# VectorE adds the fourth key tile to the sum of probabilities, and the row sums become one group of matmuls

## The chip, the cores and the metric

The kernel runs on one core of one Trainium2 chip. The metric is the device time of one execution in microseconds, as the median of the runs shown. The core has TensorE (matrix products, PE in the profile), VectorE (DVE), ScalarE (ACT), GpSimd (POOL) and the queue engine SyncE (SP), which here only starts transfers. They share the on-chip memory SBUF; matmuls write to eight accumulator banks, the PSUM (tile PS), which GpSimd does not use in this kernel.

## The reference, cut to what matters

The reference is a decoder layer over 4 sequences of 512 rows by 512 columns, in fp32: self attention, cross attention to a context of width 128 with a causal mask, and a feed-forward part with 2048 hidden columns and gelu. Each part starts with a layer norm and adds its result to x. Both attentions have 16 heads of 32 columns.

```python
q = hidden_states @ wq.T + bq          # k and v alike
scores = einsum('bhsd,bhtd->bhst', q, k) * scale
new_max = max(scores); new_exp = exp(scores - new_max)
output = einsum('bhst,bhtd->bhsd', new_exp, v) / sum(new_exp)
x = x + output @ wo.T + bo             # self attention
...
scores = where(causal, qh @ kh.T * inv_sqrt_d, min)   # cross attention
x = x + softmax(scores) @ vh @ Wout.T
x = x + gelu(layernorm(x) @ proj1.T + b1) @ proj2.T + b2
```

In self attention the loop of four ring steps sees the same keys each time, so one step gives the same result. In cross attention the causal mask leaves only the first 512 of the 1601 context rows in use.

## The kernel before

**Units.** Attention is worked in 32 units `u`: one unit is one sequence and one group of four heads (`HPG`). Units 0 to 15 are the self layer, 16 to 31 the cross layer; with four groups per sequence, `b, g = divmod(u, GROUPS)`. Projections are exact products of split operands: each fp32 operand is split into a high and a low part and `product` issues three matmuls (lines 1000 to 1002).

In a unit, TensorE makes the scores twice. `scores_for_max` (L1106) makes them with queries on the partitions, for the unit to come, and VectorE takes each row's maximum (`maximum`, L1350 in the self layer, L1356 with the mask in the cross layer). `transpose_max` (L1134) turns the maxima, `copy_max` (ScalarE, L904) puts them into the stack of queries, and `scores` (L1123, the mask at L1126) makes the scores again with keys on the partitions and the maximum subtracted. ScalarE takes the exponential into `PT` (L919). The key rows are four tiles of 128, `k` = 0 to 3. `PT` has eight slots, and tile `k` of head `h` lies in slot `(4k + h) % 8`, so tiles 2 and 3 overwrite tiles 0 and 1. In the cross layer, tile `k` holds the queries from `128k` on only.

`weigh_values` (L1139) multiplies each key tile by the values, four heads side by side in the array, and counts `p_used`. For the sum of each row of probabilities, GpSimd adds tile 0 and tile 1 of each head into `P_sum` (L783) and then tile 2 (L789). `sum_rows` then issues two groups of four heads at L1139: ones against `P_sum`, and ones against tile 3 in `PT`. VectorE's `divide` takes the reciprocal (L1364) into `oT`, which is the place of the fourth head in `P_sum`, and multiplies the weighted values by it (L1366). ScalarE (`high_output`, L892) and GpSimd (`low_output`, L773) split the result for the output projection, and GpSimd may overwrite `P_sum`'s fourth head after that.

**Order.** Each engine works in order. For TensorE, ScalarE and VectorE the order in a unit is sorted from the table `PLACES`: places in units of about a microsecond for every unit's scores, weighted values, maxima, projections' pieces (`fill`), the turn of the maxima (`body` + 1), the row sums (`body` + 2), the statistics of a coming norm, the division of the unit before, and the split of its output. `act_order`, `dve_order` and `sp_order` derive their places from TensorE's; SP's queue stores Q and K to a scratch tensor in memory and loads them back as stacks at those places. GpSimd's order is written out by hand: raw weights placed before 3.0, adds of tile 1 with `low_output` before the third, raw weights up to 9.0, adds of tile 2, the other raw weights, then the roots of the norm and the bias adds. The eight banks are dealt out in TensorE's order (`bank_fills`), with the estimates `FREED` of how long each kind is held after its place.

**Waits that matter here.** `sum_rows` waits for GpSimd's adds of the unit (`p_added`) and its last matmul counts the unit's fourth `p_used`; the division waits for it. The exponentials of tile 0 wait for the adds of the unit before, those of tile 1 for the unit before's sums (the fourth `p_used`), those of tile 2 for the adds of tile 1. VectorE's feed-forward work includes `split_hidden` (L1437, L1439), GpSimd's `ffn` bias adds at L842.

Of the kernel before, what the change touches and what calls it, by code (L numbers as in the profile page):

```python
# [7 lines left out]
BF16 = mybir.dt.bfloat16  # L8
# [4 lines left out]
P = 128  # L13
# [86 lines left out]
ADD_HEADS = {SELF: 1, CROSS: 2}  # L100


def adds_before(u):

    cross = max(u - FIRST_CROSS, 0)
    return (u - cross) * 2 * HPG + cross * (HPG + HPG // ADD_HEADS[CROSS])


def adds_until(u, k, h):

    return adds_before(u) + (h + 1 if k == 1 else HPG + h // ADD_HEADS[layer_of(u)] + 1)


BANKS = 8
FREED = dict(T=0.11, S=0.83, M=2.33, G=1.3, R=4.16, O=5.65)
# [3 lines left out]
RAW_PLACES = ((0, 0.01, 5.17, 11.56), (14.3, 22.85), (31.55,), (3.64, 24.47, 17.66, 13.33), (13.15,))  # L119
# [3 lines left out]
CHUNK_PLACES = [(25, (2.12, 13.03)), (26, (5.91, 10.57)), (28, (6.61, 7.41)), (28, (13.83, 14.58)), (29, (10.94, 19.45)), (30, (9.47, 16.47))]  # L123
# [7 lines left out]
    SELF: (dict(body=22.32,  # L131
                scores=((0.08, 0.7), (2.33, 0.39), (5.66, 1.1), (9.16, 1.52)),
                values=(4.1, 4.44, 12.02, 17.56),
                maxima=(2.5, 13.9, 18.4),
                fill=(-1.06, 13.51, 23.02),
                stats=17.28,
                divide=-2.47,
                output=3.81),
           dict(body=28.99,
                scores=((0, 0.02), (3.69, 0.66), (5.67, 1.2), (9.93, 0.32)),  # L140
                values=(5.89, 5.92, 12.1, 17.39),
                maxima=(4.36, 9.15, 16.64),
                fill=(-1.0, 11.58, 28.83),
                stats=9.24,
                divide=0.28,
                output=5.61),
           dict(body=18.49,
                scores=((1.41, 0.34), (2.65, 0.14), (7.74, 0.91), (10.49, 1.06)),
                values=(5.54, 5.81, 18.56, 18.74),
                maxima=(4.56, 9.84, 15.63),  # L150
                fill=(1.0, 9.85, 16.32),
                stats=-6.27,
                divide=0.32,
                output=3.16),
           dict(body=33.95,
                scores=((1.31, 0.22), (2.69, 0.64), (4.82, 0.87), (9.84, 1.24)),
                values=(6.17, 9.49, 11.36, 21.68),
                maxima=(3.6, 13.39, 16.85),
                fill=(1.09, 12.94, 22.75),
                stats=5.72,  # L160
                divide=0.32,
                output=4.14)),
    CROSS: (dict(body=22.71,
                 scores=((0.06, 0.51), (2.49, 0.79), (5.12, 1.59), (8.55, 0.02)),
                 values=(5.58, 8.61, 8.84, 11.87),
                 maxima=(5.17, 7.73, 19.33),
                 fill=(1.83, 10.03, 22.33),
                 stats=7.39,
                 divide=2.71,
                 output=4.29),  # L170
            dict(body=27.59,
                 scores=((0.07, 0.37), (2.29, 0.38), (5.5, 1.11), (7.82, 0.7)),
                 values=(3.5, 5.38, 11.23, 11.6),
                 maxima=(2.14, 5.48, 13.28),
                 fill=(-2.83, 7.99, 14.02),
                 stats=-5.83,
                 divide=-3.2,
                 output=3.13),
            dict(body=14.89,
                 scores=((0, 0.25), (1.66, 0.61), (6.12, 0.97), (9.01, 0.57)),  # L180
                 values=(5.23, 5.63, 10.4, 12.22),
                 maxima=(3.42, 6.65, 8.52),
                 fill=(1.35, 5.99, 9.99),
                 stats=17.22,
                 divide=-2.08,
                 output=4.37),
            dict(body=22.49,
                 scores=((0.31, 0.49), (3.27, 0.7), (5.81, 1.22), (9.1, 0.38)),
                 values=(4.96, 6.56, 15.58, 16.03),
                 maxima=(2.51, 9.81, 11.74),  # L190
                 fill=(7.67, 9.22, 15.73),
                 stats=4.37,
                 divide=0.39,
                 output=5.79)),
# [5 lines left out]
           (('Wo', 3), 'Q', ('Wo', 2), 'K'),  # L200
           ('Q', ('V', 0), 'K', ('V', 3)),
           (('V', 2), 'Q', ('V', 1), 'K')),
    CROSS: (('K', 'Q', ('Wo', 0), ('xT', 0), ('xT', 1), ('Wo', 1), ('xT', 2), ('xT', 3)),
            (('Wo', 2), ('Wo', 3), 'Q', 'K', ('V', 1)),
            ('K', 'Q', ('V', 2), ('V', 0)),
            ('Q', 'K', ('V', 3))),
# [25 lines left out]

def pe_order(u):
# [21 lines left out]
    work.append((body + 2.0, "sums", 0, 0))  # L255
# [16 lines left out]
    assert [kind for kind in kinds if kind in ("values", "sums")][-1] == "sums"  # L272
# [52 lines left out]
def dve_order(u):  # L325
# [4 lines left out]
    for place, what, which, piece in PE_ORDER[u]:  # L330
        _, _, last = use_of(u, what, which, piece)
        if what == "max":
            work.append((place, what, which))
        elif what == "sums" and u == UNITS - 1:
# [1197 lines left out]
```

## Time and profile before

| what | before |
|---|---|
| median of 3 runs | 1128.84 us (1128.45 to 1206.26) |
| the profiled execution | 1129.96 us |
| its span, first to last instruction | 1128.2 us |
| granted TensorE clock, mean | 0.999 |
| busy: TensorE, weight loads, VectorE, ScalarE, GpSimd | 97%, 68%, 60%, 42%, 38% |
| chain that ended last: TensorE, VectorE, GpSimd, ScalarE, nothing seen | 88%, 4%, 3%, 2%, 2% |

How to read it: the span is cut from the first to the last instruction of one execution. A busy share is an average over the whole span; the attention part runs from about 57 to 753 us, the feed-forward part from there to the end. Matmuls are pipelined, and the ends of the records are modelled, so the length of a group of matmuls is better read from the start of the group to the start of what follows. The chain of waits follows the work that ended last back in time.

### The profile page before, as it was taken

The numbers are of one execution on the slowest core, as the hardware profiler recorded it, in microseconds if no ns is written. First come the engines' busy times: TensorE is split into PE (matmuls) and PEld (weight loads), VectorE is DVE, ScalarE is ACT, GpSimd is POOL, SyncE is SP. The second block draws the span as 40 slices with busy tenths as digits, with TensorE's granted clock in tenths as the row PEclk, the third lists the DMA queues.
The fourth block names the chain that finished last, engine by engine and source line by source line (L and its number), as shares of the span: only waits on it lengthen the run. The fifth ranks groups of instructions, "written<-read, shape, count | busy, mean of one in ns | idle before, by whom it ended". The sixth has DMA issues, their size and how long they took to land.

```text
span 1128.2 us, 15900 instructions
## 1 busy us (share of the span) xinstructions
PE 1095.0 (97%) x5840; PEld 769.2 (68%) x5840; DVE 676.5 (60%) x1302; ACT 473.5 (42%) x792; POOL 433.4 (38%) x398
## 2 busy tenths in 40 slices
PE   5899999999999999999999999999999999999998
PEld 4656666666665665665766766667887887887886
DVE  5677667667677778778787787845433224224112
ACT  4275555446555756645555556541221111111110
POOL 1147644444456777455536476652010001001000
PEclk9999999999999999999999999999999999999999
DMA  6934243343334546445355366302201000001001
GB/s 226 284 124 126 76 140 81 101 113 113 94 94 134 146 118 168 127 141 165 107 159 175 93 183 185 86 1 84 94 19 38 1 1 37 0 0 38 1 1 38
DMA packets 73737, 110.31 MB, mean 98 GB/s; under 512 B 6976, under 2 KB 45888, under 8 KB 71744
## 3 DMA queue, kind: packets, MB, share of 16 engines
q1 hardware_dynamic: 70864, 102.00, 30.0%
q0 software_dynamic: 2080, 6.82, 2.1%
q8 instruction: 44, 0.72, 0.3%
q10 hardware_dynamic: 720, 0.54, 0.1%
q14 instruction: 29, 0.24, 0.1%
HBM read 71.58 MB, written 37.75 MB: 97 GB/s over the span
## 4 chain that ended last, share of the span: by engine, by line
PE 88%; DVE 4%; POOL 3%; ACT 2%; issue 2%; DMA 0%; DVEq 0%; SPq 0%; ACTq 0%; POOLq 0%
PE PS L1000 19%; PE PS L1001 18%; PE PS L1002 18%; PE PS L1139 12%; PE PS L1106 9%; PE PS L1123 9%; POOL P_sum L783 2%; PE PS L1030 1%; PE PS L1134 1%; ACT PT L919 1%; PE PS L1126 1%; DVE P_sum L1364 1%; POOL oTL L773 1%; DVE xnf L1308 0%; DMA x_res<-x 0%
## 5 line engine op out<-in xcount | busy, mean ns | idle before, releaser
L919 ACT ACTIVATE PT<-PS 128x512 f32<-128x512 f32 (+1 forms) x432 | 227.8, 590 | 157.3 <-PE PS L1123 61.2
L783 POOL TENSOR_TENSOR P_sum<-PT 128x512 f32<-128x512 f32 x128 | 162.0, 1285 | 251.7 <-ACT PT L919 251.6
L1350 DVE TENSOR_REDUCE m_cols<-PS 128x1 f32<-128x512 f32 x256 | 164.8, 683 | 45.2 <-PE PS L1106 44.4
L1437 DVE CAST hidH<-hid 128x512 fp32r<-128x512 f32 x64 | 30.6, 478 | 225.0 <-ACT hid L972 222.9
L1106 PE MATMUL PS<-stackK,stackQ 96*128 96x512 f32 (+3 forms) x512 | 161.5, 377 | 2.7 <-DVE stage L1322 1.7
L972 ACT ACTIVATE hid<-PS,b1c 128x512 f32<-128x512 f32 x64 | 44.0, 689 | 279.2 <-PE PS L1002 277.2
L1123 PE MATMUL PS<-stackQ,stackK 100*128 100x512 f32 (+3 forms) x512 | 158.2, 382 | 2.6 <-DVE m_cols L1356 2.5
L1356 DVE CUSTOM_DVE_ANT_0 PS<-PS,mask_qk 128x128 f32<-128x128 f32 (+3 forms) x256 | 119.3, 517 | 43.8 <-PE PS L1106 43.1
L1364 DVE RECIPROCAL P_sum<-PS 128x512 f32<-128x512 f32 x32 | 107.4, 3357 | 41.5 <-PE PS L1139 41.5
L789 POOL TENSOR_TENSOR P_sum<-P_sum,PT 128x512 f32<-128x512 f32 x96 | 121.2, 1289 | 6.0 <-ACT PT L919 1.9
L1106 PEld LDWEIGHTS PS<-stackK,stackQ 96*128 96x128 f32 x512 | 88.8, 190 | 49.6 <-issue 26.9
L1123 PEld LDWEIGHTS PS<-stackQ,stackK 100*128 100x128 f32 x512 | 92.8, 191 | 42.7 <-ACT stackQ L904 11.8
L1000 PE MATMUL PS<-xTH,FH 128*128 128x512 f32 x256 | 102.0, 398 | 0.0
L1000 PE MATMUL PS<-FH,hidH 128*128 128x512 f32 x256 | 101.3, 396 | 0.7 <-DVE hidL L1439 0.7
L1002 PE MATMUL PS<-xTH,FL 128*128 128x512 f32 x256 | 101.8, 398 | 0.0
L1001 PE MATMUL PS<-xTL,FH 128*128 128x512 f32 x256 | 101.5, 396 | 0.0
L1001 PE MATMUL PS<-FL,hidH 128*128 128x512 f32 x256 | 100.8, 394 | 0.0
L1002 PE MATMUL PS<-FH,hidL 128*128 128x512 f32 x256 | 99.6, 389 | 0.0
L1000 PE MATMUL PS<-xTH,WH 128*128 128x512 f32 x192 | 80.3, 418 | 5.1 <-DVE xTL L1314 3.6
L1001 PE MATMUL PS<-xTL,WH 128*128 128x512 f32 x192 | 76.8, 400 | 0.0
L1002 PE MATMUL PS<-xTH,WL 128*128 128x512 f32 x192 | 76.8, 400 | 0.0
L904 ACT ACTIVATE stackQ<-PS 4x1024 fp32r<-4x1024 f32 x64 | 61.6, 1008 | 34.5 <-PE PS L1134 34.1
(124 smaller groups left out, 1764.0 us busy)
## 6 DMA issues: line engine op xcount, KB each, us to landing
scratch<-stage SPq DMA_DIRECT2D x128, 256.0 KB, 2.4
stackK<-scratch SPq DMA_DIRECT2D x62, 256.0 KB, 3.9
stackQ<-scratch SPq DMA_DIRECT2D x46, 256.0 KB, 3.7
stackQ<-scratch SPq DMA_DIRECT2D x18, 512.0 KB, 4.9
stackK<-scratch SPq DMA_DIRECT2D x60, 128.0 KB, 4.0
stackQ<-scratch SPq DMA_DIRECT2D x28, 128.0 KB, 3.7
PT<-wT SPq DMA_DIRECT2D x3, 1024.0 KB, 8.6
x_res<-x SPq DMA_DIRECT2D x3, 1024.0 KB, 8.6
```

The source lines that it names most:

```text
L783: pool.tensor_tensor(P_sum[:, h, :], PT[:, h, :], PT[:, 4 + h, :], ALU.add).then_inc(p_added, 1)
L789: pool.tensor_tensor(sums, sums, PT[:, h:h + heads, q0:SEQ], ALU.add).then_inc(p_added, 1)
L919: nc.scalar.activation(PT[:, slot:slot + heads, q0:SEQ], PS[:, BANK["T", u, i], 0:heads * width].rearrange("p (h n) -> p h n", h=heads), A ...
L1000: nc.tensor.matmul(dst, wH, mH, start=first, stop=False)
L1001: nc.tensor.matmul(dst, wH, mL, start=False, stop=False)
L1002: return nc.tensor.matmul(dst, wL, mH, start=False, stop=last)
L1106: mm = nc.tensor.matmul(dst[:, a, :], stackQ[0:STACK, par, h + a, q * P:(q + 1) * P], stackK[0:STACK, par, h + a, 0:n], start=a == 0, stop ...
L1123: mm = nc.tensor.matmul(dst[:, a, :], stackK[0:STACK + HPG, par, h + a, k * P:(k + 1) * P], stackQ[0:STACK + HPG, par, h + a, q0:SEQ], sta ...
L1139: mm = nc.tensor.matmul(PS[h * HEAD:(h + 1) * HEAD, dst, q0:SEQ], lhs(h), rhs(h), start=first, stop=last)
L1350: nc.vector.tensor_reduce(m_cols[:, q, STACK + h:STACK + h + heads], bank, AX.X, ALU.max).then_inc(s_done, 1)
L1356: top = nc.vector.tensor_tensor_reduce(bank[:, a, :], bank[:, a, :], mask_qk[:, SEQ - n:SEQ], 1.0, LOWEST, ALU.add, ALU.max, m_cols[:, q, ...
L1364: nc.vector.reciprocal(oT[:, :], PS[:, BANK["R", u], :]).then_inc(r_done, 1)
```

## The change

`ADDS` and `LAST_ADDS` list the adds of both layers. GpSimd's adds are as before in number and size. A new function on VectorE, `add_last`, adds key tile 3 from `PT` to `P_sum`: one add per head in the self layer (128 x 512), one add for four heads of 128 queries in the cross layer. It waits for the exponentials and for GpSimd's third-tile add, and counts `p_all_added`. `sum_rows` issues one group, waits for `p_all_added` and counts a new semaphore, `r_full`, for which the division and GpSimd's first add of the next unit wait. The fourth `p_used` now comes from `weigh_values`. The exponentials of tile 1 wait for `p_all_added` of the unit before, too.

GpSimd's order is now sorted from places as well (`pool_order`, with the raw weights 0.6 behind ScalarE's place). All places in `PLACES`, `FREED`, `RAW_PLACES` and `CHUNK_PLACES` have new values, and the order of the fill projections in `FILL` is another one. The sums have a place of their own (`sums`), which is behind the turn in all units. Two constants change their address and their order of setting.

```diff
-ADD_HEADS = {SELF: 1, CROSS: 2}
+ADDS = {SELF: [(k, h, 1) for k in (1, 2) for h in range(HPG)],
+        CROSS: [(1, 0, 1), (1, 1, 1), (1, 2, 1), (1, 3, 1), (2, 0, 2), (2, 2, 2)]}
+LAST_ADDS = {SELF: [(0, 1), (1, 1), (2, 1), (3, 1)], CROSS: [(0, 4)]}
...
-    SELF: (dict(body=22.32,
-                scores=((0.08, 0.7), (2.33, 0.39), (5.66, 1.1), (9.16, 1.52)),
...
+    SELF: (dict(body=23.42,
+                sums=(0, 25.31),
+                adds=(0.13, 1.3, 4.19),
+                low=-0.78,
+                bo=9.67,
+                scores=((0.08, 0.7), (2.33, 0.46), (5.66, 0.78), (8.97, 1.61)),
...
+                adds=(2.36, 1.76, 2.45),
...
+                adds=(-1.2, -0.63, 2.3),
...
+                adds=(-3.33, -1.39, 1.3),
...
@@ def dve_order(u)
+    if u >= 0:
+        ends = [place for place, what, which, _ in PE_ORDER[u] if what == "scores" and T_FILLS[layer_of(u)][which][0] == KT - 1]
+        work += [(place + places["adds"][2], "add", j) for j, place in enumerate(ends)]
...
@@ GpSimd
-                for n in raws_of(u, 0.0, 3.0):
-                    low_raw(n)
-                for h in range(HPG):
-                    if u and h == 2:
-                        low_output(u - 1)
-                    add_probabilities(u, 1, h)
...
+                raws = [(RAW[n][1] + 0.6, "raw", n) for n in raws_of(u)]
+                for _, what, which in sorted(POOL_ORDER[u] + raws, key=lambda item: item[0]):
+                    if what == "add":
+                        add_probabilities(u, which)
+                    elif what == "output":
+                        low_output(which)
...
@@ exponentials (ScalarE)
+                elif k == 1 and u:
+                    act.wait_ge(p_all_added, last_adds_until(u - 1, h + heads - 1))
...
@@ sum_rows (TensorE)
-                q0 = queries(u, KT - 1)
-                pe.wait_ge(p_added, adds_before(u + 1))
+                pe.wait_ge(p_all_added, last_adds_before(u + 1))
                 take_bank(("R", u))
-                four_heads(BANK["R", u], 0, lambda h: ones[:, :], lambda h: P_sum[:, h, :], True, False)
-                four_heads(BANK["R", u], q0, lambda h: ones[:, :], lambda h: PT[:, 4 + h, q0:SEQ],
-                           False, True).then_inc(p_used, 1)
+                four_heads(BANK["R", u], 0, lambda h: ones[:, :], lambda h: P_sum[:, h, :], True, True).then_inc(r_full, 1)
...
@@ VectorE
+            def add_last(u, j):
+                h, heads = LAST_ADDS[layer_of(u)][j]
+                dve.wait_ge(p_ready, fills_until(u, KT - 1, h + heads - 1))
+                dve.wait_ge(p_added, adds_until(u, 2, h + heads - 1))
+                q0 = queries(u, KT - 1)
+                sums = P_sum[:, h:h + heads, q0:SEQ]
+                nc.vector.tensor_tensor(sums, sums, PT[:, 4 + h:4 + h + heads, q0:SEQ], ALU.add).then_inc(p_all_added, 1)
```

## Rows read from the trace of the kernel before

**Rows 1.** The page, busy time of each engine, its share and its instructions.
```profile
PE 1095.0 (97%) x5840; PEld 769.2 (68%) x5840; DVE 676.5 (60%) x1302; ACT 473.5 (42%) x792; POOL 433.4 (38%) x398
```

**Rows 2.** Table by stretches: length, busy us (instructions) per engine, clock, DMA.
```profile
57.00:77.89 20.89, 19.11 (x105) 11.99 (x103) 16.36 (x31) 14.09 (x26) 11.56 (x12) 1.00 0.51 160
77.89:753.40 675.51, 669.89 (x3972) 430.38 (x3975) 497.87 (x1003) 377.30 (x650) 386.24 (x340) 1.00 0.42 122
753.40:1128.20 374.80, 365.93 (x1614) 294.75 (x1605) 128.29 (x211) 60.21 (x87) 26.62 (x23) 1.00 0.08 26
```

**Rows 3.** Waits of PE, 77.89 to 753.40: us in total, times, longest.
```profile
PE PS L1123 <- DVE m_cols L1356: 2.5, 3, 0.8
PE PS L1030 <- ACT PT L865: 1.4, 1, 1.4
```

**Rows 4.** Table by stretches: a self batch, units 14, 15, 22 and 23.
```profile
202.51:306.67 104.16, 104.16 (x545) 67.10 (x544) 72.54 (x101) 54.95 (x93) 51.76 (x44) 1.00 0.36 102
409.41:428.98 19.57, 19.57 (x106) 11.21 (x105) 16.59 (x23) 12.80 (x23) 13.11 (x11) 1.00 0.32 106
428.98:448.60 19.62, 19.05 (x107) 10.55 (x106) 16.27 (x47) 12.39 (x22) 13.97 (x15) 1.00 0.57 146
570.51:586.79 16.28, 16.28 (x118) 10.76 (x117) 14.53 (x40) 8.80 (x16) 8.85 (x7) 1.00 0.51 167
586.79:604.03 17.24, 16.26 (x114) 10.18 (x113) 15.83 (x47) 8.92 (x16) 10.35 (x11) 1.00 0.54 150
```

**Rows 5.** Groups by line: busy us, mean ns of one, idle before.
```profile
L1139 PE MATMUL PS<-PT,ones 128*32 128x512 f32 (+1 forms) x256 | 23.1, 432 | 0.0
```

**Rows 6.** Timeline of PE, self unit 4: start us, us, engine, line, what.
```profile
170.75 1.06 PE L1139 MATMUL PS<-PT,V_odd 128*32 128x512 f32 x8
171.75 0.44 PE L1030 MATMUL PS<-ident,PT 128*128 128x128 f32 x2
...
176.90 1.06 PE L1139 MATMUL PS<-P_sum,ones 128*32 128x512 f32 x8
...
177.78 1.04 PE L1139 MATMUL PS<-PT,ones 128*32 128x512 f32 x8
...
178.75 0.50 PE L1000 MATMUL PS<-WH,oTH 128*128 128x512 f32 x1
```

**Rows 7.** Timeline of PE, cross unit 16, its row sums.
```profile
471.90 1.07 PE L1139 MATMUL PS<-P_sum,ones 128*32 128x512 f32 x8
...
472.78 0.40 PE L1139 MATMUL PS<-PT,ones 128*32 128x128 f32 x8
...
473.12 0.50 PE L1000 MATMUL PS<-WH,oTH 128*128 128x512 f32 x1
```

**Rows 8.** Lines L1281, L1439: durations ns min/median/max, first and last start, forms.
```profile
L1281 DVE TENSOR_TENSOR WL<-PT,WH x12: 680/683/686, 13.4 to 33.7; 128x512 fp32r<-128x512 f32 x12
...
L1439 DVE TENSOR_TENSOR hidL<-hid,hidH x64: 691/693/1678, 759.2 to 1118.6; 128x512 fp32r<-128x512 f32 x64
```

**Rows 9.** GpSimd against VectorE: page's group of L783, then timelines from 771 us.
```profile
L783 POOL TENSOR_TENSOR P_sum<-PT 128x512 f32<-128x512 f32 x128 | 162.0, 1285 | 251.7 <-ACT PT L919 251.6
...
771.35 5.86 POOL L842 TENSOR_TENSOR x_res<-x_res,b_b 128x512 f32<-128x512 f32 x4 [10.34 <-DMA b_b<-b]
...
772.96 1.66 DVE L1439 TENSOR_TENSOR hidL<-hid,hidH 128x512 fp32r<-128x512 f32 x1
```

**Rows 10.** Timelines of GpSimd and ScalarE, self unit 4.
```profile
161.85 5.04 POOL L789 TENSOR_TENSOR P_sum<-P_sum,PT 128x512 f32<-128x512 f32 x4
...
165.76 0.60 ACT L919 ACTIVATE PT<-PS 128x512 f32<-128x512 f32 x1 [0.97 <-PE PS L1123]
166.92 0.60 ACT L919 ACTIVATE PT<-PS 128x512 f32<-128x512 f32 x1 [0.57 <-PE PS L1123]
```

**Rows 11.** Timeline of GpSimd and PE, last unit.
```profile
751.80 1.29 POOL L789 TENSOR_TENSOR P_sum<-P_sum,PT 128x512 f32<-128x512 f32 x1
752.72 0.86 PE L1139 MATMUL PS<-PT,V_odd 128*32 128x256 f32 x16
...
753.40 1.04 PE L1139 MATMUL PS<-P_sum,ones 128*32 128x512 f32 x8
```

More of the change, by code:

```diff
@@ L122 @@
 CONSTS = 11
[L123 removed]
+CHUNK_PLACES = [(25, (5.07, 9.74)), (26, (10.86, 12.53)), (28, (7.82, 8.18)), (28, (13.83, 14.58)), (29, (14.22, 15.11)), (30, (12.56, 23.08))]
 PLACES = {
[L131 to L194 removed]
@@ L230, in first_order, with sums_of @@
     return sorted(work, key=lambda item: item[0])
+def sums_of(u):
+    return PLACES[layer_of(u)][u % GROUPS]["sums"] if 0 <= u < UNITS - 1 else (0, 99.0)
 def pe_order(u):
@@ L254, in pe_order @@
     work += [(place + t, "partial", t, piece) for unit, place, piece in PARTIAL if unit == u for t in (0, 1)]
-    work.append((body + 2.0, "sums", 0, 0))
+    for unit in (u - 1, u):
+        late, place = sums_of(unit)
+        if unit + late == u:
+            work.append((place, "sums", unit, 0))
     fill = []
@@ L271, in pe_order @@
     kinds = [item[1] for item in work]
-    assert [kind for kind in kinds if kind in ("values", "sums")][-1] == "sums"
+    if ("sums", u) in [item[1:3] for item in work]:
+        assert [kind for kind in kinds if kind in ("values", "sums")][-1] == "sums"
+    if ("sums", u - 1) in [item[1:3] for item in work]:
+        assert [kind for kind in kinds if kind in ("values", "sums")][0] == "sums"
     assert [item[2] for item in work if item[1] == "xT"] == (list(range(KT)) if g == 0 else [])
@@ L333, in dve_order @@
             work.append((place, what, which))
-        elif what == "sums" and u == UNITS - 1:
+        elif what == "sums" and which == UNITS - 1:
             work.append((place + 0.2, "divide", u))
@@ L341, in dve_order, with pool_order @@
         work += [(places["stats"] + t * 0.1, "stats", t) for t in range(KT)] + [(places["stats"] + 0.5, "moments", 0)]
+    return sorted(work, key=lambda item: item[0])
+def pool_order(u):
+    b, g = divmod(u, GROUPS)
+    places = PLACES[layer_of(u)][g]
+    at = {}
+    for place, what, which, _ in PE_ORDER[u]:
+        if what == "scores":
+            k, h, heads = T_FILLS[layer_of(u)][which]
+            for a in range(h, h + heads):
+                at[k, a] = place
+    adds = []
+    for j, (k, h, heads) in enumerate(ADDS[layer_of(u)]):
+        adds.append((max([at[k, h + heads - 1] + places["adds"][k - 1]] + [add[0] for add in adds]), "add", j))
+    work = list(adds)
+    if u > 0:
+        work.append((min(places["output"] + places["low"], adds[HPG - 1][0] - 0.01), "output", u - 1))
+    if u == 0:
+        work.append((20.0, "root", 1))
+    elif g == GROUPS - 1 and b < LAST:
+        work.append((places["stats"] + 1.5, "root", b + 2))
+    if g in (1, 2) and b < BATCH - 1:
+        work += [(places["bo"] + t, "bo", 2 * (g - 1) + t) for t in (0, 1)]
     return sorted(work, key=lambda item: item[0])
@@ L360 @@
 DVE_ORDER = {u: dve_order(u) for u in range(-1, UNITS)}
+POOL_ORDER = {u: pool_order(u) for u in range(UNITS)}
 def bank_uses():
@@ L398, in fill_of @@
     if what == "sums":
-        return ("R", u), True, True
+        return ("R", which), True, True
     if what == "up":
@@ L1120, in scores @@
                 dst = PS[:, BANK["T", u, i], 0:heads * n].rearrange("p (h n) -> p h n", h=heads)
-                cross = layer_of(u) == CROSS
+                masked = layer_of(u) == CROSS
                 for a in range(heads):
                     mm = nc.tensor.matmul(dst[:, a, :], stackK[0:STACK + HPG, par, h + a, k * P:(k + 1) * P],
-                                          stackQ[0:STACK + HPG, par, h + a, q0:SEQ], start=a == 0, stop=not cross)
-                if cross:
+                                          stackQ[0:STACK + HPG, par, h + a, q0:SEQ], start=a == 0,
+                                          stop=a == heads - 1 and not masked)
+                if masked:
                     mm = nc.tensor.matmul(dst[:, :, 0:P], identb[:, :],
@@ L1372, in in_unit @@
                         maximum(u + 1, which)
+                    elif what == "add":
+                        add_last(u, which)
                     elif what == "divide":
```

166 lines of the change are left out of this document (127 added, 39 removed).

## The prediction

> **What bounds the kernel now.** I read the page's busy shares first. TensorE is busy 1095.0 of a span of 1128.2 us [rows 1]; everything else is far below. Then the table by stretches [rows 2]: from the first row-sum matmul at 77.89 us to the last at 753.40 us, TensorE is busy 669.89 of 675.51 us, so only 5.62 us of that stretch is idle, and 1.78 us (20.89 - 19.11) in the 20.89 us before it, where the first unit runs. The waits of TensorE in that stretch [rows 3] show where idle time is left: three waits of up to 0.8 us for VectorE's cross maxima and one of 1.4 us for ScalarE's normed rows. The attention part is therefore a stream of matmuls with hardly a hole: a matmul taken out is time taken out, as long as nothing else becomes late. What could become late is read from a table by units [rows 4]. A whole batch of self units (202.51 to 306.67) has VectorE busy 72.54 of 104.16 us, 70%, with no TensorE idle at all. The last two self units have it at 85% (16.59 of 19.57) and 83% (16.27 of 19.62), a cross unit of group 2 at 89% (14.53 of 16.28), one of group 3 at 92% (15.83 of 17.24). TensorE has no hole at 89% and 0.98 us of holes at 92%: that is the scale on which I read the new VectorE work.
>
> **What goes.** The second half of the row-sum group, four heads of ones against the fourth key tile. Its busy time is 23.1 us in all [rows 5], but that is a modelled union in which ends overlap the next matmuls, so I use starts. In a self unit the pair of groups starts at 176.90 and the next matmul at 178.75, 1.85 us; a single group of the same size holds the engine from 170.75 to 171.75, 1.00 us [rows 6]. So 0.85 us goes, times 16 self units, 13.6 us. In a cross unit the pair runs from 471.90 to 473.12, 1.22 us [rows 7]; less the same 1.00 it is 0.22 us, times 16, 3.5 us. Together -17.1 us, all of it on the stream that sets the end; 23.1 is the other end.
>
> **What comes.** In self units VectorE adds the fourth tile head by head, 64 adds of 128x512; in cross units one add of four heads by 128 queries, also 512 columns, 16 of them. No row shows this add in the attention part. The nearest are VectorE's subtractions of two 128x512 operands in SBUF, 0.683 us at the start and 0.693 us in the feed-forward part [rows 8]. At 0.69, 80 adds are 55.2 us of VectorE. Most of it lies beside matmuls: a self batch goes from 72.54 to 83.58 us (16 x 0.69 more) in 104.16 - 4 x 0.85 = 100.76 us, 83%, below the 89% at which TensorE has no hole [rows 4]. So I cost these adds at nothing in the first 14 self units, covered by about 17 us of idle VectorE per batch; without that cover each costs its 0.69.
>
> The cover is thin in three places. **Units 14 and 15** (the last self units, short because their projections are few): 16.59 + 2.76 = 19.35 us of VectorE against 19.57 - 0.85 = 18.72, and 16.27 + 2.76 = 19.03 against 18.77. VectorE sets these units, which save 0.22 and 0.59 us at best; 0.9 us of the gain is given back. If VectorE also keeps its present idle time in unit 15 (3.35 us), that unit takes 22.38 us, 3.6 over 18.77, and the two give back 4.2 instead. **Cross units of groups 2 and 3** (three of each are full, units 18 to 27): with 0.69 more they stand at 15.22 of 16.06 (95%) and 16.52 of 17.02 (97%), above the 92% that has holes. I let them keep their length: 6 x 0.22, 1.3 us given back. At worst each grows by the whole add, 6 x 0.69 = 4.1 us more. **The last unit**: GpSimd's last add starts at 751.80 and lasts 1.29, to 753.09; the sums start at 753.40, straight after the weighted values [rows 11]. With an add of 0.69 between, they cannot start before 753.78, so 0.4 us is lost.
>
> **The new waits.** VectorE's add waits for GpSimd's third-tile add of the same head and for the exponentials of the fourth tile. Behind it in VectorE's queue stand the maxima (TensorE waits for their banks), the low halves of Q and K (SP's stores wait for them), V and the residual. In a self unit GpSimd's four third-tile adds run from 161.85 to 166.89, the last two exponentials of the fourth tile from 165.76 and 166.92 [rows 10]; the adds stand 1.3 to 4.19 place units (about microseconds) behind the scores, so they meet ready data for the later heads and may wait up to a GpSimd add (1.29) for the first two. That is idle time of VectorE, within the same cover: nothing. The row sums now wait for VectorE instead of GpSimd: in that unit the pair starts at 176.90, ten microseconds later, so nothing. ScalarE's second-tile exponentials wait for the previous unit's VectorE adds, but they waited for the whole previous sum group before, which comes no earlier: nothing, and a small gain at most. The division waits for the shorter group: 0.85 us earlier, no cost.
>
> **What moves.** All places are new: maxima, projections' pieces and their copies, the statistics, divisions; SP's stores and stack loads follow Q, K and scores; GpSimd's queue now interleaves the low output, the raw weights with their DMA issues, the roots and the bias adds by place instead of behind fixed groups of adds. No row prices this. Its bounds are the idle TensorE time that it could remove, 7.4 us (5.62 + 1.78), and as much that it could add, the rate of the 92% unit (0.98 of 17.24) over about seven units. The nearest row is the self batch with no hole, so I take 0. GpSimd loses no work and gains none; the constants' order and addresses lie in the start, where TensorE waits for weights.
>
> **Sum.** -17.1 + 0.9 + 1.3 + 0.4 = -14.5 us. The profiled execution took 1129.96 us (1128.2 span and 1.8 around it): 1115.5. That execution stands 1.1 us above the median of the runs, 1128.84, so the prediction is 1114.
>
> **One resource that the attention part does not show.** In the feed-forward part four GpSimd additions run back to back, 5.86 us for four where the attention's take 1.285 each; inside them VectorE's subtraction of two SBUF operands took 1.66 us instead of 0.69 [rows 8, 9]. So such an operation waits out a GpSimd one. VectorE's adds are the only such pair in the attention part; its other work there reads PSUM or a single SBUF operand. If one add in four meets GpSimd it costs 16 x 0.97 = 15.5 us of VectorE, still under the cover; I take that as nothing.
> The Trainium skill, "SBUF — State Buffer", section "SBUF: two separate sides", says that VectorE and GpSimd share a port pair by an exclusive lock which a VectorE operation with two SBUF inputs takes against a GpSimd one that reads SBUF, and that the loser fully blocks. The row at 1.66 us agrees; by the rule, were every add to collide, the sum would come out as in (c) below, 1137 instead of 1114.
>
> **Rivals.**
> (a) *The holes go too.* The new places fit the shorter stream and the 7.4 us of idle time vanish, with nothing given back: 1129.96 - 17.1 - 7.4 = 1105.5, 1104 against the median. For: the holes are few and single. Against: three recur where VectorE is fullest, and it gets fuller. Chance 0.15.
> (b) *VectorE binds at the layer change and in the cross units.* The worst prices of above: 4.2 us in units 14 and 15, 1.3 + 4.1 in the cross units, 0.4: -17.1 + 10.0 = -7.1, 1122.9, or 1122 against the median. Chance 0.15.
> (c) *Slower: the adds collide with GpSimd.* Every self add runs into a GpSimd add: 1.66 each, so a self batch has 72.54 + 26.56 = 99.1 us of VectorE in 100.76, 98%. TensorE then idles at least as at 92%, 0.98/17.24 = 5.7%, or 1.43 us per unit, 22.9 us over 16: 1138 on its own time, 1137 against the median. It decides from 0.9 us lost per self unit (14.5/16). For: a third-tile add of the next head is running just when VectorE's first may start. Against: GpSimd is free from 166.89 in a unit that lasts to 176.90, and the adds are placed late. Chance 0.08; over 2% slower would need 2.3 us per unit, chance 0.03.
> (d) *The forecast*, between 1106 and 1122: chance 0.62.
>
> **Numbers.** Prediction 1114. The range goes from the rival with no holes to a little beyond (b), 1104 to 1126; (c) and the far edge of (a) are left out. Two per cent is 22.6 us, about what a measurement of this kernel can tell from no change: faster by over 2% is under 1106.3, which needs nearly all of (a): 0.15; slower by over 2% only the far end of (c): 0.03; within: 0.82.
>
> **What would show it.** After: no matmuls of ones against the probabilities; a row-sum group about 1.0 us long; self batches of about 100.8 us; 80 adds on VectorE with a median near 0.69 us (if 1.2 to 1.7, (c)); TensorE's idle time between first and last sum near 6 us (near 0: (a); over 10: (b) or (c)); the feed-forward part unchanged at about 375 us. I am wrong if a self batch does not get 3 us shorter, or if TensorE's waits name VectorE's add.

## The result: slower by 1.5%

The changed kernel takes 1145.57 us (median of four runs, 1144.0 to 1149.65) against 1128.84 for the kernel before in the same session: ratio 1.0151, 95% interval 1.0136 to 1.0165. The 1128.84 is the median of three fast runs (1128.45 to 1129.71); a fourth fell into a slow state, took 1206.26 us and is left out. The forecast was 1114, with a range up to 1126. Its profiled execution took 1146.34 us, its span 1144.5.

The busy shares, which answer to [rows 1]:
```profile
PE 1092.0 (95%) x5584; PEld 760.8 (66%) x5584; DVE 752.1 (66%) x1382; ACT 472.6 (41%) x792; POOL 448.5 (39%) x398
```
VectorE gained 75.6 us, where 80 adds at the forecast 0.69 make 55.2, and GpSimd 15.1 us although its work is unchanged. (Records of VectorE overlap a little, so the gain is less than the 85.1 us of the adds themselves, below.) The matmuls went from 5840 to 5584.

The stretches up to the first sum, from the first to the last sum, and the feed-forward part, with the columns of [rows 2]:
```profile
57.00:78.98 21.98, 20.03 (x108) 12.55 (x106) 18.54 (x34) 14.59 (x27) 12.23 (x12) 1.00 0.46 136
78.98:771.04 692.06, 666.64 (x3723) 421.82 (x3722) 572.09 (x1080) 377.18 (x651) 400.20 (x340) 1.00 0.41 120
771.04:1144.50 373.46, 365.35 (x1606) 294.53 (x1598) 127.72 (x211) 59.70 (x86) 27.04 (x23) 1.00 0.08 26
```
The last sum starts at 771.04 instead of 753.40, 17.64 us later; the feed-forward part is 1.3 us shorter. Between the sums TensorE's idle time went from 5.62 to 25.42 us (692.06 - 666.64): it has less work and waits more.

What TensorE's matmuls waited for there, as in [rows 3]:
```profile
PE PS L1194 <- ACT PT L1007: 5.3, 8, 2.1
PE PS L1223 <- DVE m_cols L1434: 3.9, 3, 2.1
PE PS L1088 <- DVE m_cols L1440: 2.8, 3, 1.1
PE PS L1211 <- ACT stackQ L990: 2.1, 9, 0.3
PE PS L1194 <- DVE m_cols L1434: 2.0, 1, 2.0
...
PE PS L1228 <- DVE P_sum L1450: 1.1, 1, 1.1
```
L1450 is VectorE's new add, L1434 and L1440 are its maxima. The row sums (L1228) waited for an add only once. Of the 23.0 us in the whole view 11.5 name the maxima. Not all of it comes from the adds: in the kernel in which nobody adds (below) the 2.8 at L1088 are 2.6, and the 5.3 for ScalarE's exponentials are 5.0. What the adds bring are mainly the other waits for maxima, which stand behind the adds in VectorE's queue.

A self batch, units 14, 15, 22 and 23, against [rows 4]:
```profile
203.75:305.94 102.19, 101.80 (x513) 65.69 (x512) 86.83 (x117) 54.72 (x93) 54.61 (x44) 1.00 0.36 103
413.08:433.62 20.54, 19.13 (x98) 10.82 (x98) 19.67 (x27) 12.42 (x22) 13.95 (x11) 1.00 0.47 141
433.62:456.14 22.52, 19.12 (x98) 10.07 (x97) 21.47 (x53) 12.53 (x22) 17.03 (x16) 1.00 0.45 117
583.30:600.24 16.94, 16.83 (x109) 10.33 (x108) 14.80 (x40) 9.06 (x16) 8.86 (x7) 1.00 0.35 111
600.24:618.00 17.76, 16.27 (x107) 10.02 (x106) 16.78 (x48) 8.66 (x16) 10.34 (x11) 1.00 0.58 161
```
The self batch lost 1.97 us of the 3.4 that were forecast; the other four units got longer.

The adds themselves, by their line (durations in ns, minimum, median, maximum), and then the page's groups of the adds and of GpSimd's third-tile adds:
```profile
L1450 DVE TENSOR_TENSOR P_sum<-P_sum,PT x80: 674/924/4641, 69.8 to 770.3; 128x512 f32<-128x512 f32 x80
```
```profile
L881 POOL TENSOR_TENSOR P_sum<-P_sum,PT 128x512 f32<-128x512 f32 x96 | 127.3, 1350 | 6.5 <-ACT PT L1007 1.6
...
L1450 DVE TENSOR_TENSOR P_sum<-P_sum,PT 128x512 f32<-128x512 f32 x80 | 85.1, 1069 | 19.5 <-POOL P_sum L881 19.5
```
Half the adds take over 0.92 us. Of the 64 adds in self units 37 took over 0.8, and every one of these overlaps a GpSimd instruction. What that looks like, in VectorE's and GpSimd's timelines: unit 4, where GpSimd is done before the adds (163.82 + 5.04 = 168.86), and units 1 and 12, where it is not.
```profile
163.82 5.04 POOL L881 TENSOR_TENSOR P_sum<-P_sum,PT 128x512 f32<-128x512 f32 x4
...
169.25 0.68 DVE L1450 TENSOR_TENSOR P_sum<-P_sum,PT 128x512 f32<-128x512 f32 x1
```
```profile
90.27 5.97 POOL L881 TENSOR_TENSOR P_sum<-P_sum,PT 128x512 f32<-128x512 f32 x4
...
93.92 4.56 DVE L1450 TENSOR_TENSOR P_sum<-P_sum,PT 128x512 f32<-128x512 f32 x3
...
96.20 3.42 POOL L846 TENSOR_TENSOR x_res<-x_res,raw 128x512 f32<-128x512 f32 x2
98.41 0.68 DVE L1434 TENSOR_REDUCE m_cols<-PS 128x1 f32<-128x512 f32 x1
...
99.67 1.27 DVE L1434 TENSOR_REDUCE m_cols<-PS 128x1 f32<-128x512 f32 x2
...
101.00 0.64 PE L1223 MATMUL PS<-ident,m_cols 128*100 128x128 f32 x4 [2.10 <-DVE m_cols L1434]
```
```profile
372.49 5.04 POOL L881 TENSOR_TENSOR P_sum<-P_sum,PT 128x512 f32<-128x512 f32 x4
...
374.67 4.64 DVE L1450 TENSOR_TENSOR P_sum<-P_sum,PT 128x512 f32<-128x512 f32 x1
...
377.50 1.25 POOL L858 TENSOR_TENSOR WL<-raw,WH 128x512 fp32r<-128x512 f32 x1
...
379.23 1.28 DVE L1434 TENSOR_REDUCE m_cols<-PS 128x1 f32<-128x512 f32 x2
...
379.96 0.50 PE L1194 MATMUL PS<-stackK,stackQ 96*128 96x512 f32 x1 [2.00 <-DVE m_cols L1434]
```
In unit 1 three adds take 4.56 us instead of 2.1, GpSimd is slowed as well (5.97 for four instead of 5.04, its two bias adds at L846 1.71 each), the maxima come late, and the turn of the maxima (L1223) starts 2.1 us late. In unit 12 an add that starts at 374.67 lasts until 379.31, 0.56 us past the end of the fourth GpSimd instruction beside it (377.50 + 1.25 = 378.75), and the scores wait 2.0 us for the maxima behind it.

### The profile page after: what moved, and what is told of

Its sections match the earlier page's. It is cut to its first block and busy times, and to the rows that moved or that the text cites. A ratio compares the mean times of both kernels' runs of the same rounds, so it can differ in the third digit from the quotient of the medians.

```text
span 1144.5 us, 15672 instructions
## 1 busy us (share of the span) xinstructions
PE 1092.0 (95%) x5584; PEld 760.8 (66%) x5584; DVE 752.1 (66%) x1382; ACT 472.6 (41%) x792; POOL 448.5 (39%) x398
## 5 line engine op out<-in xcount | busy, mean ns | idle before, releaser
L1007 ACT ACTIVATE PT<-PS 128x512 f32<-128x512 f32 (+1 forms) x432 | 225.5, 590 | 139.8 <-PE PS L1211 51.1
L1434 DVE TENSOR_REDUCE m_cols<-PS 128x1 f32<-128x512 f32 x256 | 166.3, 683 | 30.1 <-PE PS L1194 29.5
L1194 PE MATMUL PS<-stackK,stackQ 96*128 96x512 f32 (+3 forms) x512 | 166.1, 382 | 10.7 <-ACT PT L1007 5.3
L1440 DVE CUSTOM_DVE_ANT_0 PS<-PS,mask_qk 128x128 f32<-128x128 f32 (+3 forms) x256 | 119.4, 519 | 29.0 <-PE PS L1194 28.4
L881 POOL TENSOR_TENSOR P_sum<-P_sum,PT 128x512 f32<-128x512 f32 x96 | 127.3, 1350 | 6.5 <-ACT PT L1007 1.6
L1088 PE MATMUL PS<-xTH,FH 128*128 128x512 f32 x256 | 102.0, 398 | 0.0
L1088 PE MATMUL PS<-FH,hidH 128*128 128x512 f32 x256 | 101.1, 395 | 0.0
L1450 DVE TENSOR_TENSOR P_sum<-P_sum,PT 128x512 f32<-128x512 f32 x80 | 85.1, 1069 | 19.5 <-POOL P_sum L881 19.5
L1088 PE MATMUL PS<-xTH,WH 128*128 128x512 f32 x192 | 82.7, 431 | 8.6 <-DVE xTL L1398 4.3
```

What stands on the lines that cost most here:

```text
L881: pool.tensor_tensor(sums, sums, PT[:, slot:slot + heads, q0:SEQ], ALU.add).then_inc(p_added, 1)
L1007: nc.scalar.activation(PT[:, slot:slot + heads, q0:SEQ], PS[:, BANK["T", u, i], 0:heads * width].rearrange("p (h n) -> p h n", h=heads), A ...
L1088: nc.tensor.matmul(dst, wH, mH, start=first, stop=False)
L1194: mm = nc.tensor.matmul(dst[:, a, :], stackQ[0:STACK, par, h + a, q * P:(q + 1) * P], stackK[0:STACK, par, h + a, 0:n], start=a == 0, stop ...
L1434: nc.vector.tensor_reduce(m_cols[:, q, STACK + h:STACK + h + heads], bank, AX.X, ALU.max).then_inc(s_done, 1)
L1440: top = nc.vector.tensor_tensor_reduce(bank[:, a, :], bank[:, a, :], mask_qk[:, SEQ - n:SEQ], 1.0, LOWEST, ALU.add, ALU.max, m_cols[:, q, ...
```

## The experiments

The parts are taken apart by the start of the last row sum ("last sum"), because the part after it turned out to depend on addresses. Ratios are to the kernel before, with 95% intervals.

**The new places alone.** From the changed kernel: no VectorE add, the pair of sum groups back, the new places and GpSimd's order kept.
```
-        work += [(place + places["adds"][2], "add", j) for j, place in enumerate(ends)]
...
-                four_heads(BANK["R", u], 0, ..., lambda h: P_sum[:, h, :], True, True).then_inc(r_full, 1)
+                four_heads(BANK["R", u], 0, ..., lambda h: P_sum[:, h, :], True, False)
+                four_heads(BANK["R", u], q0, ..., lambda h: PT[:, 4 + h, q0:SEQ], False, True).then_inc(r_full, 1)
```


> The changed kernel's places and its sorted GpSimd order, with the row sums as before: two groups of matmuls, no add on VectorE. Collision theory (VectorE's adds and GpSimd's operations block each other; 1.07 us mean per add instead of 0.69, one of 4.64): the places are neutral, 1126 to 1133. Occupancy theory (80 adds of 0.69 us are too much for VectorE's queue, with or without GpSimd): the same, 1126 to 1133. Places theory (the new order itself makes the holes of TensorE): 1140 or more.


1137.32 us, ratio 1.0069 (1.0049 to 1.0088), between the two expectations; last sum 762.48, 9.08 later than before. The places that the forecast put at 0 cost 9.1 us: 3.2 in the self units (unit 12 alone 29.56 instead of 27.61), 5.9 in the cross units, which grow by about 1.8 a batch (units 18 and 19: 16.94 and 17.76 instead of 16.27 and 17.25). Its stretch from the first to the last sum:
```profile
77.36:762.48 685.12, 675.90 (x3971) 429.92 (x3974) 499.65 (x1003) 376.97 (x651) 387.21 (x340) 1.00 0.41 120
```
Against [rows 2] TensorE is busy 6.0 us longer with the same matmuls and idle 3.6 us longer (9.22 against 5.62). So most of this cost is no wait: unit 18 has 117 matmuls in either order and TensorE busy all through. What in the order costs the time was not taken apart.

**The adds alone.** From the kernel before: its places, GpSimd's fixed order, a single sum group, VectorE's adds at the changed kernel's distances from the scores.
```
+ADD_AT = {SELF: (4.19, 2.45, 2.3, 1.3), CROSS: (1.3, 2.2, 5.2, 1.4)}
```


> The kernel before with its old places and its hand-written GpSimd order; only the adds on VectorE, the single sum group and the waits that belong to them are new, the adds as far behind the scores as in the changed kernel. Collision and occupancy theories: 1135 to 1155, VectorE's adds at a mean of 1 us or more under the first, 0.7 under the second. Places theory: 1112 to 1120.


1148.78 us, ratio 1.0178 (1.0156 to 1.0201); last sum 773.37. The adds on VectorE as the page has them:
```profile
L1399 DVE TENSOR_TENSOR P_sum<-P_sum,PT 128x512 f32<-128x512 f32 x80 | 83.2, 1047 | 24.8 <-POOL P_sum L814 24.8
```
They collide here as well, 1047 ns in the mean: neither the new places nor GpSimd's new order makes the collisions. The kernel is 2.3 us slower at the last sum than the changed one (773.37 against 771.04): with the adds in, the new places are better than the old.

**The same VectorE time with one operand in SBUF.** In the changed kernel's self units each add becomes statistics of the fourth tile alone, as long as an add; the fourth tile is left out of the self row sums.
```
+        junk = sb("junk", [P, KT, 6], F32)
...
-                nc.vector.tensor_tensor(sums, sums, PT[:, 4 + h:4 + h + heads, q0:SEQ], ALU.add).then_inc(p_all_added, 1)
+                if layer_of(u) == SELF:
+                    nc.vector.bn_stats(junk[:, h, :], PT[:, 4 + h, :]).then_inc(p_all_added, 1)
+                else:
+                    nc.vector.tensor_tensor(sums, sums, PT[:, 4 + h:4 + h + heads, q0:SEQ], ALU.add).then_inc(p_all_added, 1)
```


> The changed kernel, but in the self layer VectorE's add is replaced by statistics over the same 512 columns of the fourth tile: one operand in SBUF instead of two, 0.68 us, same waits, same place in the queue, same signal. It leaves the fourth tile out of the self layer's row sums. Collision theory: 0.68 us each with GpSimd beside it, GpSimd's adds back at 1.29, and 1118 to 1128. Occupancy theory: no better than 1140. Places theory: 1138 or more.


1125.49 us, ratio 0.9965 (0.9953 to 0.9977); last sum 758.41. GpSimd's adds on the page, and the new instructions in the table of groups:
```profile
L882 POOL TENSOR_TENSOR P_sum<-P_sum,PT 128x512 f32<-128x512 f32 x96 | 121.2, 1286 | 6.1 <-ACT PT L1008 1.2
```
```profile
L1452 DVE BATCH_NORM_STATS2 junk<-PT 128x6 f32<-128x512 f32 x64 | 43.6, 685 | 2.9 <-POOL P_sum L882 2.7
```
685 ns in the mean (the longest 697), GpSimd back at 1286, the last sum 12.6 us earlier than after. Same queue, same waits for data, and the length of an add that meets nothing: what costs is what the add does in SBUF beside GpSimd. The statistics differ from the add in two ways, though: they read one operand there instead of two, and they write 6 columns instead of 512. The changed kernel's own trace tells these apart. Two other groups of VectorE write 128x512 to SBUF, with one operand in SBUF and one in PSUM:
```profile
L1458 DVE TENSOR_TENSOR P_sum<-PS,P_sum x32: 691/691/692, 83.7 to 775.6; 128x512 f32<-128x512 f32 x32
```
```profile
L1409 DVE TENSOR_TENSOR stage<-PS,stage x32: 677/691/693, 413.0 to 713.1; 128x512 fp32r<-128x512 f32 x32
```
Of these 64, 26 lie beside GpSimd for more than half their time, and none takes over 693 ns. So the write is not what costs, but the two operands read from SBUF. Nor is it the tile `P_sum`, which both engines use: the adds of units 2, 6 and 10 that overlap GpSimd's bias adds alone (L846, other tiles) take 1.08 to 1.19 us. The tile "junk" (96 bytes per partition) moved the weights of the feed-forward part and made that part shorter, so a control was needed:

**The changed kernel with the same 96 bytes, unused.**
```
+        junk = sb("junk", [P, KT, 6], F32)
```


> The changed kernel with the 96 bytes per partition that the run with one operand in SBUF had added for its results, here not written by anything: all tiles behind it lie 96 bytes higher. In that run the matmuls of the feed-forward part followed each other at 227 ns instead of 232, and that part took 365.8 us instead of 373.5. If the addresses do that: 1136 to 1139, feed-forward part 366. If not: 1143 to 1147, and then all 20 us of that run were the collisions.


1138.55 us, ratio 1.0093 (1.0069 to 1.0116). Against it the one-operand kernel is 13.1 us shorter: that is the price of the collisions in the self units.

**Nobody adds.** The changed kernel without VectorE's adds, one sum group; the fourth tile is left out of the row sums of both layers.
```
-        work += [(place + places["adds"][2], "add", j) for j, place in enumerate(ends)]
...
-                pe.wait_ge(p_all_added, last_adds_before(u + 1))
+                pe.wait_ge(p_added, adds_before(u + 1))
```


> The changed kernel without any VectorE add: one sum group that waits for GpSimd's adds alone. It leaves the fourth tile out of the row sums of both layers. Collision and occupancy theories: the whole stream saving of 17 us shows, 1110 to 1116. Places theory: 1128 or more.


1131.06 us, ratio 1.0012 (0.9998 to 1.0027); last sum 757.23. The 1110 to 1116 were missed by 15 us. Against the new places alone, the single group gives 5.25 us, not 17.1: 7.2 come in the self units, and the cross units lose 1.9.

**The single group at the old places.** The kernel before without the second half of its sums; the fourth tile is left out of both layers.
```
-                four_heads(BANK["R", u], 0, lambda h: ones[:, :], lambda h: P_sum[:, h, :], True, False)
-                four_heads(BANK["R", u], q0, lambda h: ones[:, :], lambda h: PT[:, 4 + h, q0:SEQ],
-                           False, True).then_inc(p_used, 1)
+                four_heads(BANK["R", u], 0, lambda h: ones[:, :], lambda h: P_sum[:, h, :], True, True).then_inc(p_used, 1)
```


> The kernel before, with its own places, without the second half of the sum group and with nobody adding the fourth key tile (left out of the row sums of both layers): what the shorter group alone gives. By the forecast every cycle of it is time: 1129.3 - 17.1 = 1112. By the theory that the group also covers ScalarE's copy of the maxima: self units 0.87, 0.7, 0.4 and 0.25 us shorter in groups 0 to 3 (as with the late adds in the first 12 units), 16 of them about 9 us, cross units of groups 2 and 3 about nothing: last sum 9 to 10 us earlier, 1119 to 1121.


1121.03 us, ratio 0.9933 (0.9916 to 0.9949); last sum 745.42, 7.98 earlier: 6.9 in the self units, 1.1 in the cross units. Its stretch from the first to the last sum:
```profile
77.15:745.42 668.27, 656.86 (x3723) 422.14 (x3726) 498.31 (x1003) 377.97 (x650) 386.44 (x340) 1.00 0.43 123
```
Against [rows 2] TensorE's work falls by 13.0 us (669.89 - 656.86) and its idle time grows by 5.8 (5.62 to 11.41). Of the idle time 3.6 us are waits that [rows 3] does not have, of the scores for the copied maxima:
```profile
PE PS L1123 <- ACT stackQ L904: 3.6, 14, 0.4
```
Where they come from shows at the end of unit 6:
```profile
224.17 1.06 PE L1139 MATMUL PS<-P_sum,ones 128*32 128x512 f32 x8
224.27 1.93 ACT L904 ACTIVATE stackQ<-PS 4x1024 fp32r<-4x1024 f32 x2 [4.82 <-PE PS L1134]
...
225.34 0.30 PEld L1123 LDWEIGHTS PS<-stackQ,stackK 100*128 100x128 f32 x2 [1.02 <-ACT stackQ L904]
```
The sums hold TensorE from 224.17, and the scores (L1123) start at 225.34, 1.17 later instead of 1.00, when ScalarE has made the first of its two copies of the maxima (L904, half of 1.93 us each). The next pair of heads waits again for the second copy. In unit 5 the same gap is 1.45 (199.36 to 200.81); where a projection follows the sums instead (units 4 and 7) it is 1.00 and 0.99. The longer pair had covered those copies. Where the other 2 us of new idle time come from was not followed.

**Late adds, off GpSimd.** The kernel before with VectorE's adds in units 0 to 11 at places of their own, where GpSimd's third-tile adds are done; units 12 to 31 as before.
```
+SINGLE = 12
+ADD_AT = ((13.2, 14.8, 16.4, 18.0), (17.0, 18.5, 20.0, 21.5), (15.7, 16.3, 17.0, 17.7), (17.0, 18.4, 19.8, 21.2))
...
+                nc.vector.tensor_tensor(P_sum[:, h, :], P_sum[:, h, :], PT[:, 4 + h, :], ALU.add).then_inc(p_all_added, 1)
```


> The kernel before with its places; in units 0 to 11 the fourth tile is added by VectorE, head by head, but at late places, behind the maxima and behind GpSimd's own adds of the unit; units 12 to 31 keep the pair of sum groups. Collision theory: adds near 0.69 us mean, each of the twelve units 0.8 us shorter, 1119 to 1122. Occupancy theory: adds at 0.69, but no unit shorter by more than 0.3, 1127 or more.


1126.3 us, ratio 0.9978 (0.9968 to 0.9988); last sum 749.65. The adds in the table of groups:
```profile
L1389 DVE TENSOR_TENSOR P_sum<-P_sum,PT 128x512 f32<-128x512 f32 x48 | 31.3, 691 | 0.0
```
48 adds at 691 ns. Up to unit 11 the kernel is 1.05 us behind the one in which nobody adds (352.85 against 351.80): adds that don't collide are hidden almost wholly, as forecast. The expected 1119 to 1122 was missed all the same: units of groups 0 to 3 get 0.87, 0.71, 0.38 and 0.24 us shorter and not 0.8 each, since the copies of the maxima decide as in the run above, and unit 26, which keeps the pair of sums, is 1.7 us longer; why was not looked into.

**GpSimd adds the tile.** The same with the 48 adds on GpSimd.
```
+                pool.tensor_tensor(P_sum[:, h, :], P_sum[:, h, :], PT[:, 4 + h, :], ALU.add).then_inc(p_all_added, 1)
```


> As the run with late adds, but GpSimd itself does the four adds of the fourth tile in units 0 to 11 (1.29 us each, behind its third-tile adds), and VectorE does none: no collision and no VectorE time. Collision theory: 1118 to 1122. Occupancy theory: the same. If the wait of the sums for a longer chain of GpSimd matters: 1128 or more.


1131.45 us, ratio 1.0014 (1.0002 to 1.0027). The 1118 to 1122 were missed. From unit 1 on the self units are as long as with late VectorE adds; unit 0 takes 5 us more, because GpSimd's root for the second batch's norm stands behind its adds and TensorE waits 3.4 us for the normed rows.

**A piece of projection behind the sums.** Late adds, and in groups 2 and 3 of these units the last piece of the projections after the sums, to cover the copies.
```
-    work += [(body + 0.5, item) for item in fill[-TAIL:]]
+    work += [(body + (2.5 if g >= 2 and 0 <= u < SINGLE else 0.5), item) for item in fill[-TAIL:]]
```


> Late VectorE adds in units 0 to 11 as before, and in these units' groups 2 and 3 the last piece of the projections stands behind the sums instead of ahead of them, so that TensorE has work while ScalarE copies the maxima. Cover theory: units 6 and 10 get 0.45 shorter (24.82 to about 24.35), units 3, 7 and 11 0.6 (25.70 to about 25.1), together about 3 us: 1123 against 1126.3 with the late adds alone. If the copy of the maxima is not what the group covered: no change, 1126.


1131.47 us, ratio 1.0018 (1.0008 to 1.0027): not 1123 but 5 us slower than without the move. Units 6 and 10 fall to 24.54 and 24.52, but now the sums wait for VectorE's last add (seven waits, 3.5 us in all up to 360 us), units 3, 7 and 11 are 0.45 longer instead of 0.6 shorter, and units 4 and 8 are 1.7 longer, because scores wait for the bank that the division frees later. The same kernel with 96 unused bytes took 1121.7, where 1114 to 1116 had been expected.

**The same piece without any add.** The kernel with a single group at the old places (fourth tile left out), the piece moved in every group 2.


> As the kernel before with its places and the single sum group (nobody adds the fourth tile; left out of the row sums), but in every group 2 the last piece of the projections stands behind the sums instead of ahead of them. Cover theory: there the wait for the copied maxima is filled with that piece's matmuls, so units 6, 10 and 14 lose the whole 0.85 against the kernel before (25.20 to about 24.35 in units 6 and 10, where the single group alone gives 24.81 and 24.80), group 3 stays at 25.70; 1119.5 to 1120 against 1121. Rival (the second half of the sums was hidden in group 2 in some other way, in the pipeline of the matmuls): units 6 and 10 stay at 24.8, 1121.


1126.78 us, ratio 0.9978 (0.9967 to 0.9989). Unit 6's end and unit 7:
```profile
223.56 1.07 PE L1139 MATMUL PS<-P_sum,ones 128*32 128x512 f32 x8
223.66 1.93 ACT L904 ACTIVATE stackQ<-PS 4x1024 fp32r<-4x1024 f32 x2 [4.06 <-PE PS L1134]
...
224.55 0.50 PE L1000 MATMUL PS<-WH,xTH 128*128 128x512 f32 x1
...
225.35 0.85 PE L1123 MATMUL PS<-stackQ,stackK 100*128 100x512 f32 x3
...
226.15 3.35 DVE L1362 RECIPROCAL P_sum<-PS 128x512 f32<-128x512 f32 x1
...
230.88 0.64 PE L1139 MATMUL PS<-PT,V_odd 128*32 128x512 f32 x4 [0.48 <-DVE m_cols L1348]
```
The projection starts 0.99 after the sums, and the scores behind it run three in a row without a wait: the cover theory holds for that wait. But units 6 and 7 together gain only 0.18 us over the kernel without the move (50.33 against 50.51), since on VectorE the addition of V comes 1.7 later (223.84 to 225.55), the division 0.85 (225.30 to 226.15), and the weighted values of unit 7 now wait for the maxima behind them. The cross units 18 and 19 lose 1.8 together (33.32 to 35.10). The expected 1119.5 to 1120 was wrong: I had named who fills the gap, not who waits for the moved piece.

**96 unused bytes in the kernel before.**


> The kernel before with the same 96 unused bytes per partition. If the addresses set the cadence of the matmuls: 1119 to 1122, feed-forward part about 367 us instead of 374.8. If not: 1128 to 1131.


1119.01 us, ratio 0.9911 (0.9895 to 0.9928): the addresses, as expected. The stretches of this run and the next two stand in the last section.

**32 unused bytes.**


> The kernel before with 32 unused bytes per partition ahead of the feed-forward weights instead of 96: their tiles then start at a multiple of 64 bytes that is none of 128. If the feed-forward matmuls gain from a start at a multiple of 64: 227 ns apart and 1119, as with 96 bytes. If it takes a multiple of 128: 232.5 ns and 1129, as before. If it is the distance to the other operand that counts: something between.


1126.07 us, ratio 0.9971 (0.9962 to 0.9981): between the two.

**Late adds and 96 unused bytes.**


> Late VectorE adds in units 0 to 11, the rest as the kernel before, and 96 unused bytes per partition ahead of the weights of the feed-forward part. If the two gains add (1126.3 of the late adds, 10 us of the unused bytes): 1116 to 1117, below 1119.0 of the unused bytes alone. If one takes the other's place: 1119 or more.


1116.33 us, ratio 0.9885 (0.9869 to 0.9902): the gains add, and this version beats both kernels, the changed one by 29 us.

## Why the prediction was wrong

Measured at the last sum, the terms stand so:

| step | forecast, us | measured, us | from |
|---|---|---|---|
| second half of the sums goes | -17.1 | -5.3 | nobody adds against the places alone |
| VectorE's adds | +2.6 | +13.8, of it 12.6 collisions | after against nobody adds and against one operand |
| new places | 0 | +9.1 | the places alone |
| sum | -14.5 | +17.6 | 771.04 - 753.40 |

Three terms failed, and in this split none of them alone turns the sign: with only the adds as measured the sum would be -3.3, with only the single group -2.7, with only the places -5.4; any two together make it slower. The split depends on the order as well. At the old places the single group gives 8.0 us, the adds then cost 27.95 (773.37 - 745.42), and the new places with GpSimd's new order give 2.3 back; in that order the adds alone turn the sign. In either order they are the largest term.

- **The adds at nothing** is the step that failed by most. "If one add in four meets GpSimd it costs 16 x 0.97 = 15.5 us of VectorE, still under the cover; I take that as nothing." 37 of 64 met it, the 80 adds took 30.7 us more than 80 x 0.68, and one took 4.64 us beside GpSimd instructions that ran back to back. And the cover was an average of a batch: a late add holds up the maxima behind it, and those have a due time inside the unit. The mechanism was rival (c), at 0.08, and its price was close: 22.9 us for 64 collisions is 0.36 each, 12.6 for 37 is 0.34. That is in part luck: the price was worked out from how full VectorE is, the same for every unit, while 8.9 of the 12.6 us fall to units 1, 12, 15 and 16; and its 1137 still counted on the whole 17.1 us and on places at 0. Its "against" ("the adds are placed late") held only for units 4 and 8, which have no collision and are 0.89 and 0.88 shorter; unit 12, of the same group, has the add of 4.64. The rows read there [rows 10] are of such a unit; in units of groups 1 to 3, which I did not look up, the adds meet GpSimd's third-tile adds or, in 1 and 2, the bias adds behind them (in units 12 to 14 also the splitting of the weights, L858).
- **"All of it on the stream that sets the end"** failed next. At the old places 13.0 us of matmul work went, not 17.1, and 5.8 came back as waiting, 3.6 of it for ScalarE's copies: the row of unit 4, with a projection behind the sums, was taken for all units. In groups 1 and 2 the scores follow, and the end of the copy decides. The 0.85 was right where nothing waits.
- **Places taken at 0** cost 9.1 us, beyond the bound of 7.4 that I had worked out from TensorE's idle time. Idle time was the wrong measure: TensorE was busy 6.0 us longer with the same matmuls in another order, and idle 3.6 longer. Two thirds of the 9.1 lie in the cross units, nearly all of which are longer. With the adds in, though, the new places are 2.3 us better than the old; their price is that of the new order without what it was made for.
- **Units 14 and 15 bound by VectorE**: 19.35 and 19.03 us of VectorE were forecast, 19.67 and 21.47 came; the excess is again collisions (adds of 1.1 to 1.7). The units took 20.54 and 22.52. With one operand they take 19.81 and 20.65, with nobody adding 19.20 and 19.40: as forecast, added VectorE time makes these two units longer even without collisions.
- **Right**: an add by itself takes 0.68 to 0.69; 64 VectorE instructions of that length cost almost nothing (last sum 758.41 with them against 757.23 without, and the 16 cross adds are in that); the single group holds 1.0 us; the feed-forward part stays near 375; the sums hardly wait for the adds.
- **My test for being wrong** was half right: the self batch fell by 1.97 instead of 3. "TensorE's waits name VectorE's add" would have missed it: they name the maxima behind the adds.

The Trainium skill, "SBUF — State Buffer", section "SBUF: two separate sides", says that a VectorE operation with two SBUF inputs and a GpSimd one that reads SBUF exclude each other. These runs agree: 685 ns in the mean with one operand in the self units, against 1069 in the mean and 4641 at most for the 80 adds with two.

## What to carry to other kernels

Ahead of giving VectorE an operation on two SBUF operands, lay each one's due time beside GpSimd's timeline, unit by unit: here an overlap cost VectorE mostly 0.2 to 1.2 us, and once 4.0 where GpSimd's instructions ran back to back, and what counts is the work queued behind. Where work is taken from the busiest engine, look at what starts next on it and when that one's data come; if another engine's copy ends within the removed time, only the rest is gained. A new order of the same matmuls can cost the busiest engine time without any wait, so its idle time is no bound for it. A run with the new places alone and one with the new work at the old places show both prices, and that they do not simply add: here the places cost 9.1 us without the adds and gave 2.3 with them.

## What the runs showed of the hardware

It does not take two operands in SBUF to be held up by GpSimd. In the feed-forward part of the kernel before, VectorE's copy to `hidH` reads one operand and writes one, both in SBUF, and takes 428 ns in the median of 64; beside the GpSimd additions of [rows 9] it took 1.54 and 1.50 us:
```profile
L1437 DVE CAST hidH<-hid x64: 417/428/1536, 758.7 to 1118.2; 128x512 fp32r<-128x512 f32 x64
```
```profile
771.39 1.54 DVE L1437 CAST hidH<-hid 128x512 fp32r<-128x512 f32 x1 [2.10 <-PE PS L1002]
...
774.54 1.50 DVE L1437 CAST hidH<-hid 128x512 fp32r<-128x512 f32 x1
```
The statistics, which also read one operand in SBUF, were not held up (697 ns at most). What sets the two apart was not tested.

Unused bytes in SBUF changed the feed-forward part. Its stretch in the kernel before with 96 and with 32 more bytes per partition ahead of its weights, and with late adds and 96:
```profile
752.02:1119.00 366.98, 357.97 (x1614) 294.44 (x1606) 128.26 (x211) 60.26 (x87) 26.89 (x23) 1.00 0.08 27
```
```profile
752.47:1124.60 372.13, 363.35 (x1614) 294.45 (x1605) 128.20 (x211) 60.23 (x87) 26.68 (x23) 1.00 0.08 27
```
```profile
748.68:1114.70 366.02, 357.72 (x1614) 294.54 (x1606) 127.61 (x211) 60.36 (x87) 27.45 (x23) 1.00 0.08 27
```
Before it is 374.80 [rows 2]. The weights' high halves start at byte 72992 in the kernel before, 73024 with 32 bytes, 73088 with 96; only the last is a multiple of 128, and 73024 is one of 64. In the changed kernel the feed-forward matmuls start 232 ns apart in the median, with the 96 bytes 227. That it is the start address of the weights was not shown: every tile behind the unused bytes moved with them, and why 32 bytes give a part of it stays open.
